# Conditioning in half-height products, one round a block, in a fused conditioning and feed-forward kernel

## The reference, cut to what matters

```python
w = weights[conditions]                        # 128 batches pick from 200 tables of 32 x 32
h = jnp.einsum('bct,bcd->bdt', x, w)           # x: (128, 32, 256); the conditioning
logits = einsum('bsh,he->bse', h, gate_w)      # 256 -> 8
scale = top_k(logits, 2)[0].sum(-1)
s = square(relu(h @ up_w)) @ down_w            # 256 -> 1024 -> 256
y = s + (h @ expert_weight) * scale
out = x + layernorm(y) * gamma + beta
```

## Time and profile before

| what | value |
|---|---|
| runs, median (lowest to highest) | 239.31 us (238.66 to 240.37) |
| the profiled execution's own time | 238.72 us |
| its span, first to last instruction | 236.7 us |
| mean granted TensorE clock | 0.989 |
| TensorE busy with matmuls (PE) | 226.0 us, 95% |
| TensorE loading operands (PEld, beside PE) | 192.8 us, 81% |
| VectorE (DVE) | 147.1 us, 62% |
| ScalarE (ACT) | 107.2 us, 45% |
| GpSimd (POOL) | 132.0 us, 56% |

### The profile page before, as it was taken

The page is one execution under the profiler, slowest core; times in us unless marked ns, Lnnn a source line. Parts: engine busy times, 40 slices in busy tenths (PEclk is TensorE's granted clock), DMA queues, the critical chain, the costliest instruction groups (busy, mean ns, idle before and its releaser), DMA issues.

```text
span 236.7 us, 3575 instructions
## 1 busy us (share of the span) xinstructions
PE 226.0 (95%) x1250; PEld 192.8 (81%) x1250; DVE 147.1 (62%) x376; ACT 107.2 (45%) x184; POOL 132.0 (56%) x120
## 2 busy tenths in 40 slices
PE   7689999999999999999999999999999999999990
PEld 2278878888888888888888888888888888888890
DVE  1254787656667666556667666566666666666874
ACT  2248885454444444554455444544445344444100
POOL 4405696456653774465644675365745675467422
PEclk9979999999999999999999999999999999999998
DMA  5679892000200002000110002000020002000211
GB/s 188 199 228 224 173 354 76 4 1 0 83 8 0 1 0 91 1 0 0 51 40 0 3 0 89 1 3 0 15 75 3 0 0 90 3 0 0 79 56 44
DMA packets 15713, 12.95 MB, mean 55 GB/s; under 512 B 5168, under 2 KB 14896, under 8 KB 15696
## 3 DMA queue, kind: packets, MB, share of 16 engines
q1 hardware_dynamic: 15520, 12.14, 16.9%
q0 software_dynamic: 176, 0.59, 0.8%
HBM read 7.94 MB, written 4.78 MB: 54 GB/s over the span
## 4 chain that ended last, share of the span: by engine, by line
PE 85%; DMA 4%; DVE 4%; issue 3%; ACT 1%; POOL 1%; SPq 1%; POOLq 0%; DVEq 0%
PE up_ps L230 36%; PE down_ps L268 22%; PE down_ps L270 12%; PE hid_ps L217 5%; PE moe_ps L286 3%; PE moe_ps L285 3%; PE moe_ps L284 3%; DMA moe<-in_L_cond_weights_dram,cond_col 1%; DMA w_first_by_batch<-moe 1%; POOL rstd L478 1%; DMA cond_col<-in_itok_B_dram 1%; DMA wd<-w_first_by_batch 1%; PE moe_ps L217 1%; DVE hid_lo L361 1%; DVE stats L396 1%
## 5 line engine op out<-in xcount | busy, mean ns | idle before, releaser
L463 POOL TENSOR_TENSOR sq_lo<-square,sq_hi 128x512 fp32r<-128x512 f32 x64 | 83.2, 1300 | 70.6 <-DVE square L369 70.3
L268 PE MATMUL down_ps<-down_hl,sq_hi 128*128 128x512 f32 x248 | 88.7, 392 | 0.0
L270 PE MATMUL down_ps<-down_hl,sq_lo 128*128 128x256 f32 x248 | 69.6, 280 | 0.0
L369 DVE SCALAR_TENSOR_TENSOR square<-up_ps,relu 128x512 f32<-128x512 f32 x64 | 44.0, 687 | 38.2 <-ACT relu L323 38.2
L268 PEld LDWEIGHTS down_ps<-down_hl,sq_hi 128*128 128x128 f32 x248 | 46.5, 188 | 10.6
L323 ACT ACTIVATE relu<-up_ps 128x512 f32<-128x512 f32 x64 | 38.2, 597 | 34.7 <-PE up_ps L230 34.4
L230 PE MATMUL up_ps<-hid_hi,up_hi 128*128 128x512 f32 x128 | 52.2, 408 | 0.0
L230 PE MATMUL up_ps<-hid_hi,up_lo 128*128 128x512 f32 x128 | 50.3, 393 | 0.0
L270 PEld LDWEIGHTS down_ps<-down_hl,sq_lo 128*128 128x128 f32 x248 | 46.7, 188 | 2.4
L325 ACT ACTIVATE sq_hi<-relu 128x512 fp32r<-128x512 f32 x64 | 40.6, 634 | 2.0
L230 PE MATMUL up_ps<-hid_lo,up_hi 128*128 128x512 f32 x128 | 40.3, 395 | 0.5 <-DVE hid_lo L361 0.5
(11 more groups left out here) (44 smaller groups left out, 208.3 us busy)
## 6 DMA issues: line engine op xcount, KB each, us to landing
x_sb<-in_x_dram SPq DMA_DIRECT2D x8, 512.0 KB, 6.6
out_dram<-result SPq DMA_DIRECT2D x7, 512.0 KB, 2.9
result<-in_L_ffn_up_w_dram SPq DMA_DIRECT2D x2, 512.0 KB, 4.6
result<-in_L_ffn_down_w_dram SPq DMA_DIRECT2D x1, 1024.0 KB, 5.6
w_by_batch<-moe SPq DMA_DIRECT2D x1, 512.0 KB, 3.9
out_dram<-result SPq DMA_DIRECT2D x4, 128.0 KB, 1.7
wd<-w_by_batch SPq DMA_DIRECT2D x4, 96.0 KB, 5.9
eg_raw<-L_ffn_expert_weight_dram SPq DMA_DIRECT2D x1, 256.0 KB, 2.7
```

Of the source, the lines that this page charges most:

```text
L268: pe.matmul(dst[:, :], a_hi, down_hl[:, c, :, :].rearrange("p s t -> p (s t)"), start=(c == 0), stop=False)
L270: mm = pe.matmul(dst[:, T:2 * T], a_lo, down_hl[:, c, 0, :], start=False, stop=(c == CH - 1))
L369: dve.scalar_tensor_tensor(square[:, c % 2, :], up_ps[c % UPB][:, :], 0.0, relu[:, c % 2, :], ALU.max, ALU.mult).then_inc(square_done, 1)
L463: pool.tensor_tensor(sq_lo[:, j % 2, c, :], square[:, c % 2, :], sq_hi[:, j % 2, c, :].bitcast(f32), ALU.subtract).then_inc(sq_lo_done, 1)
```

## The change

Each conditioning product is cut into two. Half h takes 64 of the 128 partitions of `x_sb` and of `wd` (two batches), and 64 of the 128 columns of `wd`; the zeros that lie off those two squares are no longer multiplied. The loaded operand has 64 rows and still 128 columns, the moving operand 64 rows and 64 columns. Half 0 of all groups and of both k goes into one bank, half 1 into another, so `hid_ps` takes two banks, and `up` has three, now chosen by the running number n % 3. Both k of a block are made in one round, after c = 4 in block 0 and after c = 2 later, with one increment of `hid_done` at its end. `hidden` converts one bank h at a time, through views that put the 64 columns of each group where they belong, in the two steps after the round (c = 5 and 6 in block 0, 3 and 4 later). `up` waits at its start for both `hid_hi` parts, and before its fifth product for both `hid_lo` parts.

```diff
-UPB = 4
+UPB = 3
+PAIR = P // 2
-        hid_ps = bank("hid_ps")
+        hid_ps = ctx.enter_context(nc.psum_tensor("hid_ps", [P, 2, K, TILES, PAIR], f32))
         def round_at(j):
-            return (4, 6) if j == 0 else (2, 4)
-        def round_bank(j, k):
-            return moe_ps if j == 0 and k == 1 else hid_ps
+            return 4 if j == 0 else 2
+        def hid_sum(h):
+            return hid_ps[:, h, :, :, :].rearrange("p k t n -> p (k t) n")
+        def hid_to(buf, j, h):
+            return buf[:, j % 2, :, :].rearrange("p k (t h n) -> p (k t) h n", t=TILES, h=2)[:, :, h, :]
...
-            def conditioning(j, k):
-                if k == 0:
-                    pe.wait_ge(x_landed[j], 16)
-                    pe.wait_ge(wd_landed[min(j, 2)], 16 * Q)
-                if j > 0:
-                    pe.wait_ge(hid_lo_done, K * j + k)
-                for t in range(TILES):
-                    g = TILES * j + t
-                    mm = pe.matmul(round_bank(j, k)[:, P * t:P * t + P], x_sb[:, g, P * k:P * k + P], wd[:, g, :],
-                                   start=True, stop=True)
+            def conditioning(j):
+                pe.wait_ge(x_landed[j], 16)
+                pe.wait_ge(wd_landed[min(j, 2)], 16 * Q)
+                wait(pe, hid_lo_done, 2 * j)
+                for k in range(K):
+                    for t in range(TILES):
+                        g = TILES * j + t
+                        for h in range(2):
+                            rows = slice(PAIR * h, PAIR * h + PAIR)
+                            mm = pe.matmul(hid_ps[:, h, k, t, :], x_sb[rows, g, P * k:P * k + P],
+                                           wd[rows, g, rows], start=True, stop=True)
                 mm.then_inc(hid_done, 1)
             def up(j, c):
+                n = CH * j + c
...
                 if c == 0:
-                    pe.wait_ge(hid_hi_done, K * j + 1)
-                wait(pe, square_done, CH * j + c - UPB + 1)
-                dst, par = up_ps[c % UPB][:, :], j % 2
+                    pe.wait_ge(hid_hi_done, 2 * j + 2)
+                wait(pe, square_done, n - UPB + 1)
+                dst, par = up_ps[n % UPB][:, :], j % 2
...
-                if c == 0:
-                    pe.wait_ge(hid_hi_done, K * j + 2)
...
                 if c == 0:
-                    pe.wait_ge(hid_lo_done, K * j + 1)
+                    pe.wait_ge(hid_lo_done, 2 * j + 2)
                 product(up_hi, 0, hid_lo, 4)
-                if c == 0:
-                    pe.wait_ge(hid_lo_done, K * j + 2)
...
-            conditioning(0, 0)
-            conditioning(0, 1)
+            conditioning(0)
...
-                    if j + 1 < BLOCKS and c in round_at(j):
-                        conditioning(j + 1, round_at(j).index(c))
+                    if j + 1 < BLOCKS and c == round_at(j):
+                        conditioning(j + 1)
...
-            def hidden(j, k):
-                act.wait_ge(hid_done, K * j + k + 1)
-                act.activation(hid_hi[:, j % 2, k, :], round_bank(j, k)[:, :], ACT.Copy).then_inc(hid_hi_done, 1)
+            def hidden(j, h):
+                act.wait_ge(hid_done, j + 1)
+                act.activation(hid_to(hid_hi, j, h), hid_sum(h), ACT.Copy).then_inc(hid_hi_done, 1)
...
-                    if j + 1 < BLOCKS and c - 1 in round_at(j):
-                        hidden(j + 1, round_at(j).index(c - 1))
+                    if j + 1 < BLOCKS and c - 1 - round_at(j) in range(2):
+                        hidden(j + 1, c - 1 - round_at(j))
...
```

More of the change, by code:

```diff
@@ L224, in up, with product @@
                 if c == 0:
-                    pe.wait_ge(hid_hi_done, K * j + 1)
-                wait(pe, square_done, CH * j + c - UPB + 1)
-                dst, par = up_ps[c % UPB][:, :], j % 2
-                def product(w, k, h, n):
-                    return pe.matmul(dst, w[:, k, P * c:P * c + P], h[:, par, k, :], start=(n == 0),
-                                     stop=(n == 3 * K - 1))
+                    pe.wait_ge(hid_hi_done, 2 * j + 2)
+                wait(pe, square_done, n - UPB + 1)
+                dst, par = up_ps[n % UPB][:, :], j % 2
+                def product(w, k, h, i):
+                    return pe.matmul(dst, w[:, k, P * c:P * c + P], h[:, par, k, :], start=(i == 0),
+                                     stop=(i == 3 * K - 1))
                 product(up_hi, 0, hid_hi, 0)
@@ L322, in rectify @@
                 wait(act, square_done, n - 1)
-                act.activation(relu[:, c % 2, :], up_ps[c % UPB][:, :], ACT.Relu).then_inc(relu_done, 1)
+                act.activation(relu[:, c % 2, :], up_ps[n % UPB][:, :], ACT.Relu).then_inc(relu_done, 1)
                 act.wait_ge(relu_done, n + 1)
@@ L358, in _, with hidden @@
         def _(dve):
[L359 to L362, removed]
+            def hidden(j, h):
+                dve.wait_ge(hid_hi_done, 2 * j + h + 1)
+                dve.tensor_tensor(hid_to(hid_lo, j, h), hid_sum(h), hid_to(hid_hi, j, h).bitcast(f32),
+                                  ALU.subtract).then_inc(hid_lo_done, 1)
             def square_up(j, c):
@@ L368, in square_up @@
                 wait(dve, sq_lo_done, n - 1)
-                dve.scalar_tensor_tensor(square[:, c % 2, :], up_ps[c % UPB][:, :], 0.0, relu[:, c % 2, :],
+                dve.scalar_tensor_tensor(square[:, c % 2, :], up_ps[n % UPB][:, :], 0.0, relu[:, c % 2, :],
                                          ALU.max, ALU.mult).then_inc(square_done, 1)
@@ L466, in add_beta @@
             def add_beta(j, half):
-                pool.wait_ge(hid_done, K * j + K)
+                pool.wait_ge(hid_done, j + 1)
                 if j == 0 and half == 0:
```

## The result

The changed kernel takes 244.57 us (median of 4 runs, 243.73 to 245.43), the kernel before 239.55 us in the runs beside it. The ratio is 1.0217 with a 95% interval of 1.0177 to 1.0257: slower by 5.0 us, where +4.0 and 243.0 us had been forecast. The four runs lie in two pairs, 243.7 and 243.8 us with a mean granted clock of 0.980, and 245.4 us twice with 0.974 and 0.975, and the profiled execution is one of the lower pair. Its span is 241.6 us for 236.7: 4.9 us more, and every part of that can be read from TensorE's starts.

What follows compares the result with a forecast made beforehand. TensorE was taken as the bound, with matmuls filling 95% of the span. The terms 0 + 3.9 + 0.9 - 0.8 = +4.0 us gave 242.7 to 243.3, stated as 243.0 us; range 234 to 257.

Steps and rivals of the forecast that it cites:

- The stream of products: TensorE's 32 matmuls a block: a pair of halves costs 0.111 us, 1.78 us a block as before, so 0.
- Into the halves and out of them: TensorE around each round: the array must empty at each switch, 0.28 us each, 0.55 a block, +3.9 us in all.
- The start: Block 0: both conversions wait for one increment, so up(0, 0) starts at about 17.2 us; +0.9 us.
- The wait for hid_lo: End of block 0: the second hid_lo comes earlier, so up(1, 0) no longer waits for it; -0.8 us.
- the rest of `down_w`: Second half of down(0, 0): named as what is late next, ready at 36.47 us and just met.
- Three banks, views, one increment: Fewer banks for up, views of hidden in runs of 64, one increment for two: slack or free time hides them, 0.
- one way in and out free: Low end of the forecast's own range: part of the cost of switching into and out of halves absent, 240.5 us.
- the late clock: High end of the forecast's own range: clock climbs later at the start, six products cost up to 1.4 us more, 245.5.
- Rival A: Conditioning rounds: the halves truly halve the cost, -3.9 us, 234.9, or 231 with no switching cost; chance 0.27.
- Rival B: Conditioning rounds: loads go one behind another, 3.55 us a block, +19.8 us, 258.5, or 256 with earlier clock rise; chance 0.22.
- Rival C: Nothing changes: a pair at 0.111 us with free switching, +0.1 us, 239.0, or 0.08 with full switching cost; chance 0.19.

Runs made afterwards that it cites:

- two_rounds: The changed kernel, but blocks 2 to 7 make their two k in two rounds of 16 matmuls, after c = 1 and c = 2: 247.03 us.
- halves apart: The changed kernel with the same 32 products a round, all of half 0 ordered before all of half 1: 261.29 us.
- beta_late: The changed kernel with the two add_beta of block 0 moved behind that block's last split_square on GpSimd: 242.91 us.
- before_warm: The kernel before with 38 warm-up matmuls for 26: 239.08 us, ratio 1.0004 to the kernel before.
- full_one_round: The changed kernel's schedule (one round, three banks for up, later conversions) with full-height products as in the kernel before: 242.31 us.

## Why the prediction came out, point by point

**The stream of products: 0 forecast, 0 measured.** The pair of halves costs 0.111 us by two kernels (two_rounds and the changed one). The reason given was right as well, and each side of it was shown apart: the halves overlap (halves apart: 0.104 for 0.060), the moving columns are not the limit (32 columns: 1.91 for 1.93), the load is (full height with 64 moving columns: still 0.110; loads of 64 columns: 0.059 within a quarter, 0.017 for all four together). The estimate from the load's durations at the two clocks, 93 to 111 ns, holds both direct measurements, 0.104 and 0.110. Its reading of the bf16 load of 151 ns as the low clock's fits the trace of before, where these loads stand 0.43 us apart up to 6.1 us, twice as far as later; the column of the granted clock shows 1.00 there all the same. The Trainium skill ("TensorE: Matmul & The Clock Gate", section LDWEIGHTS) has the load's time go by columns and not by rows; the runs agree, with 0.104 us for 64 rows and 0.110 for 128.

**Into the halves and out of them: 3.9 forecast, 2.5 to 2.7 measured.** 0.36 us for a way in and a way out (two_rounds), 0.38 a block by the distance, for 0.55. The cost exists and has the cause named in part: the load path stands idle 0.24 us, and no load goes in early. That the array must be empty first is not shown, since the first matmul of a round starts at 72.03, before the recorded end of the `down` matmul at 72.11. The size was off: I let the last matmul run to its recorded end, 275 ns, and added the whole lead of a load. The first matmul of a round in fact starts with its load, at 72.03, only 0.08 us after its usual place at 71.95. The Trainium skill ("TensorEngine Tiling (Array Packing)", section Key Properties) has a change of mode drain the engine; the rows show a price for it, 0.36 us for two changes, but not that it is a drain.

**The start: +0.9 forecast, +1.9 measured.** This is the mis-sized term on the other side. `up(0, 0)` came at 16.43, not 17.2, as the round was shorter (2.83 us for 3.3) and began at 12.33 for 12.60, which is chance; with the high clock `up(0, 2)` would have stood at 16.43 + 12 x 0.232 + 0.73 = 19.94, 0.14 later than before. The low clock lasted to 20 us and cost the other 1.76. I had seen the idle time fall where the clock climbs, priced it at up to 1.4, and set it at 0. The kernel with 38 warm-up matmuls, 2.2 us earlier at `up(0, 2)`, shows that the clock's price belonged in the sum.

**The wait for hid_lo: -0.8 forecast, -0.8 measured.** Exact, and the next wait was looked for in the wrong place: I named the rest of `down_w`; it was GpSimd's `sq_lo`, +1.07 us, a term that the sum had at nothing. I had not followed GpSimd's queue in block 0, where `add_beta` stands between two `split_square` and waits for its transfers. Moving the two `add_beta` (beta_late) takes the wait away, and making everything else earlier (before_warm) brings it into the kernel before.

**Three banks, views, one increment: 0 forecast, 0 measured** in blocks 1 to 7 (26.96 for 26.94 in full_one_round).

So the sum was right to 1 us with two errors of opposite sign: 1.2 to 1.4 too much for the ways in and out, 2.1 too little in block 0. That they nearly cancelled is luck; that the stream of products costs nothing more or less is not. Two ends of the forecast's own range do not follow from its terms: one way in and out free would give 243.0 - 1.95 = 241.1 and not 240.5, and the late clock 243.0 + 1.4 = 244.4 and not 245.5.

Rival A had a pair of halves at half the price, 0.055 us; it is 0.111. Rival B had halves that don't overlap, 3.55 us a round; it is 1.93. Rival C had the ways in and out free; they cost 0.36 us. All three are excluded by the runs.

## What to carry to other kernels

Before splitting a small product over parts of the array, ask which of its two streams is the limit: here a float32 load of 128 columns held its part of the array for 0.10 to 0.11 us, with 128 rows or 64, and with 128, 64 or 32 columns moving past it. Splitting the rows alone doubled the loads and gave nothing; splitting the loaded columns too made four quarters run together. Collect such products into one round, since each way in and out cost 0.36 us, let neighbours lie in different parts of the array, and when a wait is taken away, follow every engine's queue for the next one, the slow ones and their transfers first.

## What the runs showed of the hardware that was not expected

- 64 loads and matmuls of 64 x 64 with 64 moving float32 columns take 1.09 us with the way in: 0.017 us for a load and a matmul.
- The order of the same 32 half-height calls is worth 1.4 us a round (3.32 against 1.93): the halves overlap where neighbours lie in different ones.
- A TensorE without a gap can lose its clock: in halves_apart, where all products of half 0 come before all of half 1, the granted clock fell to 0.50 for about 3 us behind three of the rounds, and about 1.5 us was lost each time. The later rounds of that kernel at 78.10 and 197.56 us did not do it, and what decides between them is open.
- With TensorE idle from 14.6 to 15.9 us, after a warm-up that ran up to the first round, the granted clock stayed at 1.00; with an idle stretch of 2.6 us before the round it fell to half at 13.3 us and came back at 20.
